# Routing tags of 39 expert tiles: one load during the attention in place of one small load per tile

## The reference

```python
xn = layernorm(x)
# attention: 16 heads of 32, causal, then a projection
attn = attention(xn, w_attn, b_attn) @ w_proj + b_proj
# experts: 8 of them, 512 -> 2 x 352 -> 512, two per token
probs = softmax(xn @ gate_w.T)
topw, sel = top_k(probs, 2); topw /= topw.sum(-1)
h = silu(xn @ w1_gate[e]) * (xn @ w1_up[e])      # for each chosen expert e
ffn = sum over the two chosen e of topw_e * (h @ w2[e])
out = x + attn + ffn
```

## Time and profile before

| what | value |
|---|---|
| time, median of 3 runs | 934.96 us (934.89 to 943.35) |
| the profiled execution's own time | 937.0 us |
| its span | 935.1 us |
| TensorE busy | 829.9 us, 89% of the span |
| VectorE, ScalarE, GpSimd busy | 515.4, 395.0, 272.6 us |
| mean granted TensorE clock | 0.949 of full speed |

### The profile page before, as it was taken

How to read it: one execution, slowest core, us unless ns; L and a number is a source line. 1 busy time by engine, 2 the same in 40 slices (tenths; PEclk the granted TensorE clock), 3 DMA queues, 4 the chain that set the end, 5 groups by cost and what they waited for, 6 DMA issues and landing times. The chain is left out here.

```text
span 935.1 us, 13836 instructions
## 1 busy us (share of the span) xinstructions
PE 829.9 (89%) x3973; PEld 561.9 (60%) x3974; DVE 515.4 (55%) x1334; ACT 395.0 (42%) x779; POOL 272.6 (29%) x352
## 2 busy tenths in 40 slices
PE   3889999289989999999999999798989889899990
PEld 3678988254545555555554444576767667677760
DVE  5983453584566666666674021664656546666640
ACT  3321221014545555555655400454545545455630
POOL 3781000405132342423331510032323323333330
PEclk9999999758899999999999999998999999999995
DMA  9386596867356576676730138434454453633336
GB/s 318 142 262 206 202 312 203 250 164 227 97 155 165 175 182 165 182 189 178 196 100 14 41 103 275 161 68 137 73 151 120 100 149 67 160 68 67 68 35 200
DMA packets 76717, 143.21 MB, mean 153 GB/s; under 512 B 12928, under 2 KB 26752, under 8 KB 76608
## 3 DMA queue, kind: packets, MB, share of 16 engines
q10 hardware_dynamic: 29056, 58.28, 22.7%
q1 hardware_dynamic: 38192, 65.68, 22.7%
q0 software_dynamic: 9424, 18.69, 9.9%
HBM read 81.21 MB, written 61.15 MB: 152 GB/s over the span
## 5 line engine op out<-in xcount | busy, mean ns | idle before, releaser
L1342 ACT ACTIVATE probs<-scores_t 128x512 f32<-128x512 f32 (+3 forms) x384 | 163.8, 492 | 148.0 <-PE scores_t L1469 136.1
L895 DVE TENSOR_TENSOR w_lo<-w,w_hi 128x704 fp32r<-128x704 f32 x156 | 131.6, 884 | 121.3 <-ACT w_hi L826 115.7
L1446 PE MATMUL maxima<-k_stack,q_stack 96*128 96x512 f32 (+3 forms) x384 | 142.4, 391 | 15.2 <-DMA q_stack<-qk_hi 9.1
L1489 PE MATMUL o_acc<-probs,v_ones 128*64 128x512 f32 (+3 forms) x768 | 149.1, 511 | 0.0
L1469 PE MATMUL scores_t<-q_stack,k_stack 98*128 98x512 f32 (+3 forms) x384 | 138.3, 385 | 7.3 <-DMA q_stack<-row_lo 5.2
L1376 DVE TENSOR_REDUCE mx<-maxima 128x1 f32<-128x512 f32 x128 | 88.2, 689 | 88.4 <-PE maxima L1446 88.2
L1372 DVE CUSTOM_DVE_ANT_0 masked_scores<-maxima,mask_m 128x128 f32<-128x128 f32 (+3 forms) x256 | 121.6, 485 | 24.2 <-PE maxima L1446 21.1
L958 PE MATMUL down<-w,hidden_t 128*128 (+1 forms) x234 | 114.8, 628 | 20.7 <-DVE hidden_t L882 20.7
L826 ACT CAST w_hi<-w 128x704 fp32r x156 | 114.0, 782 | 34.7 <-issue 33.5
L940 PE MATMUL gu<-w_hi,rows_hi 128*128 128x352 f32 x312 | 120.6, 386 | 5.3 <-DVE rows_lo L888 4.0
L1469 PEld LDWEIGHTS scores_t<-q_stack,k_stack 98*128 98x128 f32 x384 | 73.5, 194 | 69.3 <-issue 42.1
(11 more groups left out here) (158 smaller groups left out, 1175.7 us busy)
## 6 DMA issues: line engine op xcount, KB each, us to landing
w<-in_w_t SPq DMA_DIRECT2D x8, 1408.0 KB, 6.4
routed<-blank_row ACTq DMA_DIRECT2D x20, 514.0 KB, 7.2
rows<-routed ACTq DMA_DIRECT2D x39, 256.0 KB, 3.6
qk_hi<-st_hi SPq DMA_DIRECT2D x32, 256.0 KB, 4.7
qk_lo<-st_lo SPq DMA_DIRECT2D x32, 256.0 KB, 6.1
q_stack<-qk_hi ACTq DMA_DIRECT2D x32, 256.0 KB, 4.0
k_stack<-qk_hi ACTq DMA_DIRECT2D x26, 256.0 KB, 4.7
v_all<-o_t SPq DMA_DIRECT2D x4, 1536.0 KB, 5.7
```

The source lines that it names most:

```text
L895: nc.vector.tensor_tensor(w1_lo[r][:, k, :], w1_rows(slot, k), as_f32(w1_hi[r][:, k, :]), ALU.subtract).then_inc(w1_done, 1)
L1342: nc.scalar.activation(probs[:, k % PR, h, 0:w], scores_t[e % RING][:, 0:w], ACT.Exp).then_inc(exp_done, 1)
L1446: nc.tensor.matmul(mb[at % RING][:, 0:w], q_st[i][0:3 * HD, h, t * P:(t + 1) * P], k_st[i][0:3 * HD, h, c * CH:c * CH + w], start=True, st ...
L1489: last = nc.tensor.matmul(o_acc[c][2 * HD * h:2 * HD * (h + 1), CH - w:CH], v_st[i][:, j, h:h + 2, :].rearrange("p o d -> p (o d)"), probs ...
```

## The change

A tile `tags` of 128 x 39 x 2 numbers lives through the whole program. SP fills it with one DMA in round 9 of the attention, right behind the bias load, after a wait until all 32 scatters have landed. In the expert stage ACT takes the weight from `tags`, without a wait for a tag. GpSimd copies the row number of the next tile into a double-buffered column `row_index`, in the place of the one-column operation that stood there, and the indirect DMA takes its row numbers from there. The 39 loads of single tags and their two semaphores are gone. The order in which the weight pieces are made is not touched.

```diff
@@ experts
-        tag = m.sbuf("tag", [P, 2, XW - D], F32)
+        tags = keep["tags"]
-        carrier = m.sbuf("carrier_y", [P, 2], F32)
+        row_index = m.sbuf("row_index", [P, 2], F32)
@@ experts, gpsimd
-            def load_tag(i, r):
-                pool.dma_start(tag[:, r:r + 1, :], in_rows[bass.ds(i, 1), :, D:XW].rearrange("a p d -> p a d")).then_inc(tag_in[r], 16)
+            def tag_of(i):
+                return tags[:, bass.ds(i, 1), 0:1].rearrange("p o n -> p (o n)")
+
+            nc.gpsimd.tensor_copy(row_index[:, 0:1], tag_of(0)).then_inc(carried, 1)
             def tile(i, r, half):
                 pool.wait_ge(y_read, i + 2)
                 if past(i, 1):
                     pool.wait_ge(added, i * 16)
-                if past(i, 2):
-                    pool.wait_ge(carried, i - 1)
-                nc.gpsimd.tensor_tensor(carrier[:, r:r + 1], ident[:, 0:1], ident[:, 0:1], ALU.mult).then_inc(carried, 1)
+                pool.wait_ge(carried, i + 1)
+                after = i if isinstance(i, int) and i == SLOT_TILES - 1 else i + 1
+                nc.gpsimd.tensor_copy(row_index[:, 1 - r:2 - r], tag_of(after)).then_inc(carried, 1)
                 pool.indirect_dma_start(out=scratch["acc"], out_offset=bass.IndirectOffsetOnAxis(
-                    ap=tag[:, r, 0:1].bitcast(U32), axis=0), in_=y[:, r, :], in_offset=None, compute_op=ALU.add).then_inc(added, 16)
-                if not (isinstance(i, int) and i == SLOT_TILES - 1):
-                    load_tag(i + 1, 1 - r)
-            load_tag(0, 0)
+                    ap=row_index[:, r:r + 1].bitcast(U32), axis=0), in_=y[:, r, :], in_offset=None, compute_op=ALU.add).then_inc(added, 16)
@@ experts, scalar: y_to_sbuf
                 act.wait_ge(y_full, i + 1)
-                act.wait_ge(tag_in[r], half * 16 + 16)
                 if not early(i):
                     act.wait_ge(added, i * 16 - 16)
-                nc.scalar.activation(y[:, r, :], down[r][:], ACT.Copy, scale=tag[:, r, 1:2]).then_inc(y_read, 1)
+                nc.scalar.activation(y[:, r, :], down[r][:], ACT.Copy, scale=tags[:, bass.ds(i, 1), 1:2].rearrange("p o n -> p (o n)")).then_inc(y_read, 1)
@@ attend, sync
                 if n == BIAS_ROUND - 1:
                     sp.dma_start(bp[:], b_proj.partition_broadcast(P)).then_inc(bp_in, 16)
+                    sp.wait_ge(scattered, 16 * TOPK * NT)
+                    sp.dma_start(keep["tags"][:], scratch["routed"][0:SLOT_TILES * P, D:XW].rearrange("(a p) d -> p a d", p=P)).then_inc(tags_in, 16)
...
             sort_out(ROUNDS - 1, NC - 1)
+            sp.wait_ge(tags_in, 16)
```

More of the change, by code:

```diff
@@ L709, in experts @@
         rows_in = [m.sem(f"rows_in{r}") for r in range(2)]
-        tag_in = [m.sem(f"tag_in{r}") for r in range(2)]
         acc_started = keep["acc_started"]
@@ L1083, in attend @@
         proj_banks = scores_t + mb
-        scattered = m.sem("scattered")
+        scattered, tags_in = m.sem("scattered"), m.sem("tags_in")
         w_proj_in = m.sem("w_proj_in")
@@ L1558, in attention_and_experts @@
             "tile_slot": m.sbuf("tile_slot", [1, SLOT_TILES], I32),
+            "tags": m.sbuf("tags", [P, SLOT_TILES, XW - D], F32),
             "acc_started": m.sem("acc_started"),
```

## The result

The changed kernel takes 909.19 us (median of 4 runs, 906.29 to 910.05); the kernel before took 938.18 us beside it (4 runs, 934.89 to 943.35). The ratio is 0.9677, with a 95% interval of 0.9636 to 0.9718. The forecast was 906.0 in 900 to 914, from a median of 934.96 that three runs had given; the forecast gain was 29.0 us, the difference of the two medians now is 938.18 - 909.19 = 28.99. That the two agree to 0.01 us is luck: the interval of the ratio leaves 26.5 to 34.1 us of 938.18, and the two profiled executions lie 937.0 - 906.29 = 30.7 us apart. The span is 904.6 against 935.1.

What follows compares the result with a forecast made beforehand. TensorE, busy 89% of the span, bounds the kernel; its idle time and lower clock can be won. Expert stage 28.3 + end 1.0 - attention 0.3 = 29.0 us; 934.96 - 29.0 = 906.0 us, range 900 to 914.

Steps and rivals of the forecast that it cites:

- The expert stage: Expert stage: the wait for the tag goes; gain 28.3 us, the middle of 29.3 and 27.3.
- The way from above: Expert stage: 36 tiles at 7.27 us, as where no tag is late, take 261.7 instead of 291.05; gain 29.3 us.
- The way from below: Expert stage: idle time 19.9, clock 5.8 and slower down products after waits 1.6 us; together 27.3 us gained.
- The end: Last tile: the last add goes out 0.5 to 1.4 us earlier, then waits for tile 37's add; 1.0 us gain taken.
- The attention: Round 9: the load of all tags may make share_rows late, costing between nothing and 3 us, once; 0.3 us taken.
- The slack: Expert stage, path from y to next down product: about 0.5 us, from y 3.7 us late against 3.17 us idle.
- the next path binds: Rival, expert stage: ACT and DVE exceed the slack, each tile takes 7.5 us, total 913 us; chance 0.12.
- The weight load finds another victim: Rival, expert stage: the rows' load or the add becomes as late as the tag was; 929 to 930 us; chance 0.04.
- The load of all tags blocks SP's queue: Rival, attention: at 157 ns a packet, round 10's rows leave 34 us late; 940 us; harmful from 142 ns; chance 0.04.

Runs made afterwards that it cites:

- single loads put back: Changed kernel with the 39 single loads back on GpSimd, read by nobody: ratio 0.9685 without a wait, 1.0104 with ACT's y waiting for its tile's load.
- three tiles ahead: Changed kernel without the big load, 39 single loads on GpSimd's queue issued three tiles ahead, y waiting for them: ratio 0.9664 to the kernel before.
- the wait kept: Changed kernel with single loads put back and read by nobody, ACT's y waiting for its tile's load: 948.04 us, ratio 1.0104 to the kernel before.

## Why the prediction was right, and which terms were off

**The step that carried it** was that y's wait for a tag is the wait that ends last in the expert stage, and that its delay passes through `w_hi`, `w_lo` and `hidden_t` to TensorE. The pair of runs with the single loads put back shows it: the same loads, the same copy, and only the wait between them; 260.7 against 298.05 us. Putting the wait's data on another road (three tiles ahead) gives all but 1.4 us of the stage's gain without the change's big load.

**The sizes.** The expert stage: 28.3 us forecast, 30.35 measured. The way from above was the better one: 7.27 a tile forecast, 7.24 measured, 29.3 and 30.35. The way from below, 27.3, had the idle time right (19.9, measured 19.92), but the busy time was stretched by 10.4 us and not by 5.8 + 1.6 = 7.4. By groups of instructions the down product's busy time fell from 114.8 to 108.0 us over the program, 6.8 us, near the forecast, and that of the up product's three groups from 323.9 to 322.5, which I had left out; together 8.2. The other 2.2 us lie in how matmuls follow each other, and no row parts them. Taking the middle of the two ways gave away 2 us. The end: 1.0 forecast, 1.0 measured, with the cause forecast: the wait for the tag became one for the add of tile 37. The attention: 0.3 forecast, 0.6 to 1.7 measured over rounds 9 to 11, inside the bounds of 0 to 3, so the choice of 0.3 was too low; `share_rows` and with it `scale_span` were 0.7 us later. Profile against profile the sum is 30.35 + 1.0 - 1.0 (the first down product at 607.88 for 606.88) and 0.1 behind the last add, which gives the 30.5 us between the spans. The 28.3 was too low by 2 us and the cost of the attention by up to 1.4; these errors, and the scatter of the medians, let the forecast of 29.0 meet 28.99.

**The slack** of the path from y to the next down product was put at 0.5 us; it is about 0.1. The prediction set two things against each other that do not compare. Its lateness of 3.7 us was counted from the end of the down product, but y starts some 0.25 us behind that end when nothing is late (646.80 to 647.03 in the rows above). And the idle time of 3.17 us is not all that the tile grew by: 732.63 - 721.94 = 10.69 is 3.45 us more than 7.24. The lateness less that quarter of a microsecond is 3.44 too. Nothing in the sum hung on the slack, since the register instruction ahead of y takes 60 ns in the changed kernel's trace. But that the change stayed at 7.24 was nearer luck than the prediction knew: the rival "the next path binds" was given 0.12 on a slack that was not there, and by the same sums (an estimate) a y that is 0.3 us later would have made every tile 0.2 us longer.

**The rivals.** *The weight load finds another victim*: it did find one, the add of tile 13 landed after 8.7 us, and it had some 4 us of slack (forecast 4.3). *The load of all tags blocks SP's queue*: 9.6 ns a packet, far from 142; yet the queue is blocked for 5.5 us when the load stands at the wrong place. *The next path binds* at 7.5 us a tile: 7.24 measured, and this path by itself takes 7.15. The 7.5 us that two tiles with a short wait took before match the loop over the tag's load (7.5) and not this path.

## What to carry to other kernels

A load of a few bytes that is asked for one step before its use is a loop over its landing time, however small it is: compare the loop's length (here 7.5 us) with the bounding engine's time per step (7.24), and ask what it becomes beside a big load (2.64 + 7.9 + 0.1, some 11 us). The cure is to ask earlier, in one load or in many; the traffic of the small loads was not the cost. Then add up the loop that comes next in the same way, piece by piece (here 7.15 us), and don't read its slack off one late step. To size such a gain, take the distance between steps where nothing is late and multiply, and don't add up idle times alone: a third of the gain here was that the same instructions were busy for less time.

## What the runs showed of the hardware

The clock did not fall behind every long wait, and the length of the wait alone does not decide it. In the kernel before, the six matmuls took 5.48, 4.54 and 4.27 us after 3.43, 3.28 and 3.60 us of idle time, but 2.84 after 3.17, and 2.84 after 3.33, which is longer than 3.28:

```profile
808.22 2.84 PE L958 MATMUL down<-w,hidden_t 128*128 x6 [3.33 <-DVE hidden_t L882]
```

In the run with only the load added they took 2.84 after 3.28 us and 4.34 after 3.31; with the wait kept in the changed kernel they took 4.25 and more after all of 3.31 to 3.64. The Trainium skill's page "TensorE: Matmul & The Clock Gate", section "Part 1: The HAM clock gate", describes the fall to the lower level after idle time. What decides between 3.28 and 3.33 us no run here shows.

And 4992 packets of 8 bytes on SP's queue cost 9.6 ns each, 3.0 us of each DMA engine, but far more from issue to landing: 6.9 to 10.0 us in the seven runs that load them at the head of round 9, 10.1 ahead of the rows of round 10, 5.1 at the end of the attention. What makes it 6.9 in one run and 10.0 in another at the same place is not shown.
